# An audio tower on one core: all matmuls on half rows and 32 columns, each half in a PSUM bank of its own, in windows of one exp

## The chip, the cores and the metric

The kernel runs on one core of a Trainium2 chip. The metric is device time in microseconds, the median of several runs; the profile is of one execution. TensorE (PE) multiplies matrices into PSUM, which has 8 banks of 128 partitions x 512 float32. ScalarE (ACT) computes the exponentials, VectorE (DVE) and GpSimd (POOL) the rest, SyncE (SP) issues most DMAs. The engines run beside each other and meet at semaphores.

## The reference

Eight waveforms of 120000 samples go through three layers. `inputs` of the first are frames of 80 samples, 1500 a waveform. Its core:

```python
h = jnp.einsum('bfr,hr->bfh', x, W) + b            # 80 -> 256, then layer norm with gamma, beta
h = gelu_erf(layernorm(h) * ln_gamma + ln_beta)    # "_L0_tok_ref"
h = h + attention(_layernorm(h))                   # 16 heads of 16, 1500 x 1500 scores, Wq Wk Wv Wo, biases
h = h + ffn(_layernorm(h))                         # "_L0_ffn_ref"
```

The last layer would gather 8 // 16 = 0 tokens per head (the leading length, 8, over its 16 heads), so all that is left of it is a layer norm: h + layernorm(layernorm(h)) * ln_g + ln_b. Both kernels compute it so.

## The kernel before

**Tiling.** A batch has 1500 tokens in NT = 12 tiles of T = 125. A chunk is 500 tokens (QC), so NC = 3. A unit is four heads (HG) and one chunk of queries: NU = 12 units a batch, 96 in all. A unit computes, for each of the 12 key tiles and four heads, 125 keys x 500 queries of scores (`scores`, L823; float16 halves of q and k, 64 rows a head, written to a DRAM scratch and read back by `load_group`, L248), their exp on ACT (L486, L489, L494, two heads or 1000 columns each), and the sum with the values (`attend`, L852; float32, 125 rows, four heads in four blocks of 32 columns). Half of each block holds a column of ones, so the row sums come along. No maximum is subtracted unless a check at run time (`take_flag`) asks for a second pass with `exact_max`; with these inputs it isn't run.

**Tiles of the array.** Scores run on 64 rows x 32 columns of the array, in two row halves and four column blocks, eight matmuls a pair of heads. Everything else runs on 128 (125) rows x 32 columns, four matmuls, apart from the transposes (128 x 128). A float32 matmul stands in the trace as two matmul records.

**Rounds.** A unit has PER = 8 rounds of three exps. Scores use banks 0 to 5, three pairs. PE issues three pairs of scores, each after the exp that frees its banks, then one attend (even rounds) or two (odd rounds), then a piece of the next batch or of the last one (`beside`, L860). Attends of unit n go to bank 6 + n % 2, pieces to the other of the two, after DVE has copied out the sums there (`take_sums`, L607).

**Pieces.** A table written by hand (`place`, L37 to L87) says in which unit and round each runs. For the batch after: six token pairs (`tok`, 80 to 256), six transposes of z (`turn`), twelve query or key blocks (`qk`, two halves each), twelve value tiles (`val`), three norm sums (`norm`), one `flag`. For the same or the last batch: twelve output row tiles (`out`). Each has a taker on DVE in the same order: `tok_stats` and `tok_norm` (L513, L522), `take_turn`, `take_qk` (L560), `take_val`, `take_norm`, `take_out` (L625) with its `finish_out` (L635) after the next piece or at the unit's end. Between the two POOL computes the reciprocal root (`out_root`, L382). A piece waits until the piece before it has left its bank (`s_free`).

**Around it.** A unit's sums go from `Osb` by DMA to `thin`, are inverted (`invert`, L613), go back into `Den`, multiply the rest (`normalise`, L617) and go by four DMAs into `oT`. In unit 2, round 2, ACT changes its table and runs the gelu of the whole next batch. Before the loop batch 0's projections run alone; after it the last eight output tiles.

The three exps of a round, and the order of the attends:

```python
act.activation(prob[0:T, 6 * p:6 * p + 2, :], PS[0:T, 0:2, 0:QC], ACT.Exp, scale=scl)
...
if r % 2 == 0:
    attend(n, 3 * q)
else:
    attend(n, 3 * q + 1)
    pe.wait_ge(s_ex, at(s_ex, 3 * R + 3))
    attend(n, 3 * q + 2)
used = beside(b, u, r, bank, used)
```

## Time and profile before

| | us |
|---|---|
| median of 3 runs (2450.72 to 2453.55) | 2451.26 |
| the profiled execution | 2454.76 |
| its span, first to last instruction | 2453.0 |
| first exp to last exp | 117.0 to 2399.1 |
| PE busy (matmuls) | 2220.3 |
| ACT busy | 2153.5 |
| DVE busy | 920.1 |
| POOL busy | 370.5 |

A matmul's time in the trace runs from its start until its last column has left the array, so matmuls that stream side by side or behind each other overlap, and busy PE isn't PE at its peak. Consecutive exps overlap too: each is some 1.0 us long. What one engine can do per unit of time is read from starts, not from lengths. "Idle before" at a line names the engine whose signal ended the idle time. The granted TensorE clock is 0.97 of full speed over the whole span, and 1.00 in most of the loop.

### The profile page before, as it was taken

To read this page: it belongs to the slowest core of one execution; us is meant where nothing else is said; L and a number is where in the kernel's file an instruction comes from. 1 tells how busy PE (TensorE), PEld (TensorE's weight loads), DVE (VectorE), ACT (ScalarE), POOL (GpSimd) and SP (SyncE) were. 2 spreads that over 40 slices of the span, in tenths; PEclk is the share of its full clock that TensorE was granted. 3 is DMA by queue.
4 is the path that set the end of the run, shared out by engine and by line. 5 is a ranking of instruction groups with operands and counts; after the bars stand their busy time and mean duration, and the time that the engine had idled before them with its cause. 6 is when DMAs were issued, how large, how long until landed. Compare 5 with 4: busy or idle time off the path is not lost.

```text
span 2453.0 us, 75572 instructions
## 1 busy us (share of the span) xinstructions
PE 2220.3 (91%) x33324; PEld 613.4 (25%) x33324; DVE 920.1 (38%) x2075; ACT 2153.5 (88%) x2332; POOL 370.5 (15%) x495
## 2 busy tenths in 40 slices
PE   4589999999999999999999999999999999988892
PEld 1222222222222222222222222222222222222221
DVE  7442235532354234533345233542335332330114
ACT  0098999989999899998999899998999989999991
POOL 2211002211021111210112110211112111110002
PEclk7799999999999999999999999999999999999996
DMA  2311221222112222212212221222222122111101
GB/s 71 107 38 40 60 74 41 58 66 67 45 47 67 64 69 49 59 49 59 74 42 51 73 63 45 51 59 64 70 55 51 42 66 69 47 45 39 34 7 32
DMA packets 110030, 135.39 MB, mean 55 GB/s; under 512 B 32263, under 2 KB 89670, under 8 KB 109694
## 3 DMA queue, kind: packets, MB, share of 16 engines
q1 hardware_dynamic: 107158, 128.64, 20.9%
q8 instruction: 264, 4.33, 0.7%
q10 hardware_dynamic: 2536, 1.83, 0.3%
q14 instruction: 72, 0.59, 0.1%
HBM read 55.16 MB, written 61.44 MB: 48 GB/s over the span
## 4 chain that ended last, share of the span: by engine, by line
issue 49%; PE 21%; ACT 14%; POOL 8%; DVE 3%; DMA 2%; POOLq 1%; SPq 1%; DVEq 0%; ACTq 0%
PE PS L856 9%; ACT prob L489 6%; PE PS L830 6%; ACT prob L486 5%; PE PS L790 4%; POOL sq L380 2%; POOL Y L388 2%; ACT prob L494 2%; POOL rs L390 2%; DMA qk_halves_scratch<-HL 1%; SPq L246 1%; DVE HL L568 1%; DVE HL L566 1%; POOLq L389 1%; DVE z L550 1%
## 5 line engine op out<-in xcount | busy, mean ns | idle before, releaser
L856 PE MATMUL PS<-prob,Vst 125*32 125x500 f32 x9216 | 1131.2, 593 | 0.2 <-ACT prob L489 0.2
L494 ACT ACTIVATE prob<-PS 125x1000 f32<-125x1000 f32 x768 | 776.7, 1011 | 133.9 <-PE PS L830 131.8
L486 ACT ACTIVATE prob<-PS 125x1000 f32<-125x1000 f32 x768 | 776.4, 1011 | 80.4 <-PE PS L830 80.4
L830 PE MATMUL PS<-QA,KA 64*32 64x500 f16 (+1 forms) x18432 | 751.9, 381 | 97.5 <-ACT prob L489 48.8
L489 ACT ACTIVATE prob<-PS 125x1000 f32<-125x1000 f32 x768 | 786.7, 1024 | 0.0
L830 PEld LDWEIGHTS PS<-QA,KA 64*32 64x32 f16 (+1 forms) x18432 | 200.5, 90 | 907.3 <-ACT prob L486 416.2
L856 PEld LDWEIGHTS PS<-prob,Vst 125*32 125x32 f32 x9216 | 218.7, 108 | 431.2 <-issue 241.7
L566 DVE TENSOR_SCALAR HL<-PS,b_qk 128x500 f16<-128x500 f32 x96 | 70.9, 738 | 502.9 <-PE PS L790 426.8
L790 PE MATMUL PS<-zT,w_qk 128*32 128x500 f32 x1536 | 197.4, 596 | 9.0 <-DVE Osb L611 7.5
L380 POOL TENSOR_TENSOR sq<-HL 128x2000 bf16<-128x2000 f16 x24 | 84.5, 3520 | 751.4 <-DVE HL L568 751.4
L611 DVE COPY Osb<-PS 128x500 f32<-128x500 f32 x96 | 64.9, 677 | 256.7 <-PE PS L856 256.7
L819 PE MATMUL PS<-w_o,oT 128*32 128x256 f32 (+1 forms) x1536 | 102.5, 388 | 37.1 <-DMA oT<-On 22.4
L799 PE MATMUL PS<-w_v,zT 128*32 128x256 f32 (+1 forms) x1536 | 104.3, 395 | 21.8 <-DVE Vst L573 20.9
L385 POOL TENSOR_SCALAR rs<-mv 125x1 f32<-125x1 f32 x96 | 25.7, 268 | 595.1 <-DVE mv L633 594.5
L623 DVE TENSOR_TENSOR On<-Den,Osb 128x500 f32<-128x500 f32 x96 | 103.7, 1080 | 7.9 <-issue 0.9
L629 DVE TENSOR_TENSOR Hs<-Hs,PS 125x256 f32<-125x256 f32 x96 | 39.6, 413 | 166.2 <-PE PS L819 166.2
L790 PEld LDWEIGHTS PS<-zT,w_qk 128*32 128x32 f32 x1536 | 48.2, 113 | 130.0 <-issue 100.6
L642 DVE SCALAR_TENSOR_TENSOR Y<-Hs,rs,Y 125x256 f32<-125x256 f32 x96 | 72.9, 759 | 7.2
L517 DVE BATCH_NORM_STATS2 st<-PS 125x6 f32<-125x256 f32 x96 | 36.5, 422 | 102.9 <-PE PS L774 102.9
L819 PEld LDWEIGHTS PS<-w_o,oT 128*32 128x32 f32 (+1 forms) x1536 | 46.2, 111 | 113.7 <-issue 36.9
L568 DVE SCALAR_TENSOR_TENSOR HL<-PS,b_qk,HL 128x500 f16<-128x500 f32 x96 | 70.9, 739 | 7.9 <-issue 0.9
L573 DVE TENSOR_TENSOR Vst<-PS,b_v 125x256 f32<-125x256 f32 x96 | 40.1, 421 | 88.5 <-PE PS L799 88.5
(79 smaller groups left out, 961.5 us busy)
## 6 DMA issues: line engine op xcount, KB each, us to landing
qk_halves_scratch<-HL SPq DMA_DIRECT2D x384, 125.0 KB
QA<-qk_halves_scratch SPq DMA_DIRECT2D x64, 375.0 KB, 5.2
KA<-qk_halves_scratch SPq DMA_DIRECT2D x64, 375.0 KB, 7.4
oT<-On SPq DMA_DIRECT2D x384, 31.2 KB, 2.0
out<-Y SPq DMA_DIRECT2D x24, 500.0 KB
X<-in_x SPq DMA_DIRECT2D x8, 468.8 KB, 8.0
thin<-Osb SPq DMA_DIRECT2D x96, 7.8 KB
Den<-thin SPq DMA_DIRECT2D x96, 7.8 KB
```

Of the source, the lines that this page charges most:

```text
L380: pool.tensor_tensor(sq[:, :, :], HL[:, :, 0, :], HL[:, :, 0, :], ALU.mult).then_inc(s_sq, 1)
L486: act.activation(prob[0:T, 6 * p:6 * p + 2, :], PS[0:T, 0:2, 0:QC], ACT.Exp, scale=scl)\
L489: act.activation(prob[0:T, 6 * p + 2:6 * p + 4, :], PS[0:T, 2:4, 0:QC], ACT.Exp, scale=scl)\
L494: act.activation(prob[0:T, 6 * p + 4:6 * p + 6, :], PS[0:T, 4:6, 0:QC], ACT.Exp, scale=scl)\
L566: dve.tensor_scalar(HL[:, i % 4, 0, :], PS[:, bank, 0:QC], bias, None, ALU.add)
L568: dve.scalar_tensor_tensor(out=HL[:, i % 4, 1, :], in0=PS[:, bank, 0:QC], scalar=bias, in1=HL[:, i % 4, 0, :], op0=ALU.add, op1=ALU.subtra ...
L623: dve.tensor_tensor(On[:, :], Den[:, :], Osb[:, :], ALU.mult).then_inc(s_on, 1)
L790: ins = pe.matmul(PS[lo:hi, bank, 0:QC], w_qk[:, c, w, m * 128 + lo:m * 128 + hi], zT[:, c, :], start=(c == 0), stop=(c == KC - 1))
L799: last = pe.matmul(PS[lo:hi, bank, 0:D], zT[:, c, t + lo:t + hi], w_v[:, c, :], start=(c == 0), stop=(c == KC - 1))
L819: last = pe.matmul(PS[lo:hi, bank, 0:D], oT[:, m, e * T + lo:e * T + hi], w_o[:, m, :], start=(m == 0), stop=(m == KC - 1))
L830: last = pe.matmul(PS[lo:hi, bank, 0:QC], KA[rows, G % 2, h // 2, t * T + lo:t * T + hi], QA[rows, G % 2, h // 2, c * QC:(c + 1) * QC], st ...
L856: last = pe.matmul(PS[lo:lo + 2 * HD, 6 + n % 2, 0:QC], Vst[:, b % 2, t, g * HG + j, :], prob[0:T, (HG * t + j) % 12, :], start=(t == 0), ...
```

## The change

Every product that had 125 or 128 rows is cut into rows 0 to 63 and the rest (token frames into 40 samples with the bias row, and 40 from partition 64 on, so `X` and `w_tok` get a second part). Each half writes a bank of its own, four column blocks each, and DVE adds the two banks. Transposes, norm sums and the flag stay as they were. The scores keep their form.

PSUM is divided anew: scores have two pairs of banks (0 to 3) in place of three, attends of unit n use the pair 4 + 2 (n % 2), pieces the other pair.

A unit has WIN = 24 windows, one for each exp. In window k PE waits for exp k - 1, issues the scores of exp k + 1, then in even windows one attend (k // 2 - 1; the unit's last attend is in window 0 of the next unit), in odd windows at most one step of a piece. A token pair, value or output tile has two steps two windows apart, a query or key block four, of half the columns and half the depth each. The table of pieces is new, by window. ACT's wait on `s_pv` is one for every second exp.

On DVE `take_sums`, `invert` and `normalise` stand at windows 1, 7 and 12, `finish_out` three windows after its tile's last step, or at the unit's end. `take_qk` has four operations in place of two and a semaphore of its own (`s_hl`) for the stores and POOL's squares. After the loop the finish of a tile comes behind the take of the next.

```diff
+    RH = RF // 2
...
-    PER = 8
-    assert NU == NT and NT * HG == 6 * PER and KR == 64
...
+    WIN = NT * HG // 2
...
+    OFFSETS = {"tok": (0, 2), "turn": (0,), "qk": (0, 2, 4, 6), "val": (0, 2), "norm": (0,), "flag": (0,), "out": (0, 2)}
+    PLAN = {(u, k): [] for u in range(NU) for k in range(WIN)}
+
+    def place(u, what, *at):
+        for k, i in at:
+            for step, off in enumerate(OFFSETS[what]):
+                PLAN[u, k + off].append((what, i, step, off == OFFSETS[what][-1]))
+
+    place(0, "out", (3, 3), (13, 4), (19, 5))
+    place(0, "tok", (9, 2))
+    place(1, "tok", (3, 3), (15, 4))
+    place(1, "out", (7, 6), (11, 7), (19, 8))
+    place(2, "tok", (3, 5))
+    place(2, "out", (9, 9), (13, 10), (19, 11))
+    place(3, "turn", (3, 0), (5, 1))
+    place(3, "qk", (7, 0), (15, 1))
+    place(4, "qk", (3, 2), (11, 3))
+    place(4, "val", (19, 0))
+    place(5, "val", (3, 1), (7, 2), (11, 3), (21, 4))
+    place(5, "turn", (15, 2), (17, 3))
+    place(5, "norm", (19, 0))
+    place(6, "qk", (3, 4), (11, 5))
+    place(6, "val", (19, 5))
+    place(7, "qk", (3, 6), (11, 7))
+    place(7, "val", (19, 6))
+    place(8, "val", (3, 7), (21, 8))
+    place(8, "turn", (7, 4), (9, 5))
+    place(8, "norm", (11, 1))
+    place(8, "qk", (13, 8))
+    place(9, "qk", (3, 9), (11, 10))
+    place(9, "val", (19, 9))
+    place(10, "qk", (3, 11))
+    place(10, "val", (11, 10), (15, 11))
+    place(10, "tok", (19, 0))
+    place(11, "norm", (3, 2))
+    place(11, "out", (5, 0), (11, 1), (15, 2))
+    place(11, "flag", (9, 0))
+    place(11, "tok", (19, 1))
...
+    NORMS = {(2, 18): 0, (4, 2): 1, (6, 2): 2}
+    GELU = (2, 12)
+
+    TAKE, INVERT, NORMALISE = 1, 7, 12
...
+    def pair(use):
+        if use < FIRST:
+            return 2 * (use % 4)
+        if use < LAST:
+            return 4 + 2 * ((UNIT_OF[use] + 1) % 2)
+        return 2 * ((use - LAST) % 3)
...
-                sp.wait_ge(s_free, at(s_free, USE["qk", b, i] + 1))
+                sp.wait_ge(s_hl, at(s_hl, b * 4 * NC + i + 1))
...
+                        if k == TAKE and n > 0:
+                            spread_sums(n - 1)
+                        if k == INVERT and n > 0:
+                            gather_sums(n - 1)
+                        if k == NORMALISE and n > 0:
+                            store_attended(n - 1)
...
-                            act.wait_ge(s_sc, at(s_sc, 3 * R + 1))
-                            if Q > 0:
-                                act.wait_ge(s_pv, at(s_pv, 3 * Q if p else 3 * Q - 2))
-                            act.activation(prob[0:T, 6 * p:6 * p + 2, :], PS[0:T, 0:2, 0:QC], ACT.Exp, scale=scl)\
-                               .then_inc(s_ex, 1)
-                            act.wait_ge(s_sc, at(s_sc, 3 * R + 2))
-                            act.activation(prob[0:T, 6 * p + 2:6 * p + 4, :], PS[0:T, 2:4, 0:QC], ACT.Exp, scale=scl)\
-                               .then_inc(s_ex, 1)
-                            act.wait_ge(s_sc, at(s_sc, 3 * R + 3))
-                            if Q > 0 and not p:
-                                act.wait_ge(s_pv, at(s_pv, 3 * Q - 1))
-                            act.activation(prob[0:T, 6 * p + 4:6 * p + 6, :], PS[0:T, 4:6, 0:QC], ACT.Exp, scale=scl)\
+                            act.wait_ge(s_sc, at(s_sc, w + 1))
+
+                            if w >= 6 and w % 2 == 0:
+                                act.wait_ge(s_pv, at(s_pv, w // 2 - 2))
+                            act.activation(prob[0:T, 2 * (w % 6):2 * (w % 6) + 2, :],
+                                           PS[0:T, 2 * (w % 2):2 * (w % 2) + 2, 0:QC], ACT.Exp, scale=scl)\
                                .then_inc(s_ex, 1)
 
             second[0] = False
...
+            def tok_stats(b, i):
+                p, e, (upper, lower) = i % 2, hslot(b, 2 * i), two(USE["tok", b, i], slice(0, T), 2 * D)
                 dve.wait_ge(s_full, at(s_full, USE["tok", b, i] + 1))
+                h = Hs[:, e:e + 2, :].rearrange("p a d -> p (a d)")
+                dve.tensor_copy(h, upper)
+                dve.drain()
+                dve.tensor_tensor(h, h, lower, ALU.add).then_inc(s_free, 1)
...
+                upper, lower = two(USE["qk", b, i], slice(0, 128), QC)
+                dve.tensor_scalar(tmp[:, i % 2, :], upper, bias, None, ALU.add)
+                dve.drain()
+                dve.tensor_tensor(tmp[:, i % 2, :], tmp[:, i % 2, :], lower, ALU.add).then_inc(s_free, 1)
+                dve.drain()
+                dve.tensor_copy(HL[:, i % 4, 0, :], tmp[:, i % 2, :])
+                dve.drain()
+                dve.tensor_tensor(HL[:, i % 4, 1, :], tmp[:, i % 2, :], HL[:, i % 4, 0, :], ALU.subtract).then_inc(s_hl, 1)
...
+                dve.tensor_tensor(v, upper, b_v[:, :].rearrange("p (h d) -> p h d", d=HD), ALU.add)
+                dve.drain()
+                dve.tensor_tensor(v, v, lower, ALU.add).then_inc(s_free, 1)
...
-                dve.tensor_copy(Osb[:, :], PS[:, 6 + n % 2, 0:QC]).then_inc(s_ov, 1)
+                bank = 4 + 2 * (n % 2)
+                dve.tensor_copy(Osb[:, :], PS[:, bank, 0:QC])
+                dve.drain()
+                dve.tensor_tensor(Osb[:, :], Osb[:, :], PS[:, bank + 1, 0:QC], ALU.add).then_inc(s_ov, 1)
...
+                dve.tensor_tensor(h, h, upper, ALU.add)
+                dve.drain()
+                dve.tensor_tensor(h, h, lower, ALU.add).then_inc(s_free, 1)
...
+                finish = []
+                for k in range(WIN):
+                    if k == TAKE and n > 0:
+                        take_sums(n - 1)
+                    if k == INVERT and n > 0:
+                        invert(n - 1)
+                    if k == NORMALISE and n > 0:
+                        normalise(n - 1)
+                    if b + 1 < B and (u, k) in NORMS:
+                        norm_stats(b + 1, NORMS[u, k])
+                        norm_apply(b + 1, NORMS[u, k])
+                    for what, pb, i, step, last in pieces(b, u, k):
...
+                            finish.append((k + 3, pb, i))
...
+                    if finish and finish[0][0] == k:
+                        finish_out(*finish.pop(0)[1:])
+                for due, pb, i in finish:
+                    finish_out(pb, i)
...
+            def halves(n):
+                return enumerate((slice(0, 64), slice(64, n)))
...
+                for r, rows in enumerate((slice(0, RH + 1), slice(64, 64 + RH))):
                     for lo, hi in blocks(T):
-                        last = pe.matmul(PS[lo:hi, bank, j * D:(j + 1) * D], X[:, 2 * i + j, lo:hi], w_tok[:, :],
-                                         start=True, stop=True)
...
+                a, c, w, m = step // 2, step % 2, (i % 4) // 2, i % 2
+                if step == 0:
+                    pe.wait_ge(s_free, at(s_free, USE["turn", b, 2 * (i // 4) + 1] + 1))
+                cols = slice(a * QC // 2, (a + 1) * QC // 2)
+                for r, rows in halves(128):
+                    for lo, hi in blocks(128):
+                        last = pe.matmul(PS[lo:hi, bank + r, cols], w_qk[rows, c, w, m * 128 + lo:m * 128 + hi],
+                                         zT[rows, c, cols], start=(c == 0), stop=(c == 1))
...
-                b, g = n // NU, (n % NU) // NC
-                for j in range(HG):
-                    lo = 2 * HD * j
-                    last = pe.matmul(PS[lo:lo + 2 * HD, 6 + n % 2, 0:QC], Vst[:, b % 2, t, g * HG + j, :],
-                                     prob[0:T, (HG * t + j) % 12, :], start=(t == 0), stop=(t == NT - 1))
+                b, g, bank = n // NU, (n % NU) // NC, 4 + 2 * (n % 2)
+                if t == 0:
+                    pe.wait_ge(s_free, at(s_free, UNIT_USES[n]))
+                    if n > 1:
+                        pe.wait_ge(s_ov, at(s_ov, n - 1))
+                for r, rows in halves(T):
+                    for j in range(HG):
+                        lo = 2 * HD * j
+                        last = pe.matmul(PS[lo:lo + 2 * HD, bank + r, 0:QC], Vst[rows, b % 2, t, g * HG + j, :],
+                                         prob[rows, (HG * t + j) % 12, :], start=(t == 0), stop=(t == NT - 1))
...
+                for k in range(WIN):
+                    w = WIN * n + k
+                    if w > 0:
+                        pe.wait_ge(s_ex, at(s_ex, w))
+                    if k < WIN - 1:
+                        scores(w + 1, exact_max)
+                    elif not exact_max and n + 1 < B * NU:
+                        if (u + 1) % NC == 0:
+                            pe.wait_ge(s_ld, at(s_ld, 64 * ((n + 1) // NC + 1)))
+                        scores(w + 1, False)
+                    if k % 2:
+                        beside(b, u, k)
+                    elif k:
+                        attend(n, k // 2 - 1)
+                    elif n > 0:
+                        attend(n - 1, NT - 1)
+
```

Two places in the engines' queues; numbers count an engine's rows. First PE in batch 0, where the query and key blocks of batch 1 begin (before: unit 3, rounds 2 and 3; after: unit 3, windows 6 to 8). "32x500 x3" and "29x500" together are one head's scores, L830 before, L873 after. Before:

```order
468 L856 MATMUL PS<-prob,Vst 32x500 x4
469 L790 MATMUL PS<-zT,w_qk 32x500 x4
470 L830 MATMUL PS<-QA,KA 32x500 x3
471 L830 MATMUL PS<-QA,KA 29x500
...
481 L830 MATMUL PS<-QA,KA 29x500
482 L856 MATMUL PS<-prob,Vst 32x500 x8
483 L790 MATMUL PS<-zT,w_qk 32x500 x4
484 L830 MATMUL PS<-QA,KA 32x500 x3
```

After:

```order
564 L903 MATMUL PS<-prob,Vst 32x500 x8
565 L873 MATMUL PS<-QA,KA 32x500 x3
566 L873 MATMUL PS<-QA,KA 29x500
...
568 L873 MATMUL PS<-QA,KA 29x500
569 L828 MATMUL PS<-zT,w_qk 32x250 x8
570 L873 MATMUL PS<-QA,KA 32x500 x3
...
573 L873 MATMUL PS<-QA,KA 29x500
574 L903 MATMUL PS<-prob,Vst 32x500 x8
```

Before, six heads' scores (rows 470 to 481), three exps' worth, stand between one lump of attends (L856) and half a block (L790) and the next. After, it is two heads' scores, then either an attend (L903, eight matmuls) or a quarter of a block (L828).

Second DVE at the start of unit 1 of batch 1 (batch 1 is the first with outputs of an earlier one), from the sums on. Before, with `take_sums` at L611, a token pair at L517 to L533:

```order
292 L611 COPY Osb<-PS 128x500
293 L517 BN_STATS st<-PS 125x6 x2
294 L519 BN_AGGR mv<-st 125x2
295 L520 BN_AGGR mv<-st 125x2
296 L526 SCALAR_TENSOR_TENSOR Hs<-PS,mv,g_tok 125x256 x2
297 L533 SCALAR_TENSOR_TENSOR Hs<-Hs,rs,be_tok 125x256 x2
...
303 L615 RECIPROCAL thin<-thin 100x20
...
309 L619 STREAM_SHUFFLE Den<-Den 128x500
310 L623 TENSOR_TENSOR On<-Den,Osb 128x500
311 L629 TENSOR_TENSOR Hs<-Hs,PS 125x256
```

After, with the sums at L631 and L633, a token pair at L526 to L545, an output tile from L652 on:

```order
409 L631 COPY Osb<-PS 128x500
410 L633 TENSOR_TENSOR Osb<-Osb,PS 128x500
411 L526 COPY Hs<-PS 125x512
412 L528 TENSOR_TENSOR Hs<-Hs,PS 125x512
413 L531 BN_STATS st<-Hs 125x6 x2
414 L533 BN_AGGR mv<-st 125x2
415 L534 BN_AGGR mv<-st 125x2
416 L540 SCALAR_TENSOR_TENSOR Hs<-Hs,mv,g_tok 125x256 x2
417 L545 SCALAR_TENSOR_TENSOR Hs<-Hs,rs,be_tok 125x256 x2
418 L637 RECIPROCAL thin<-thin 100x20
419 L652 TENSOR_TENSOR Hs<-Hs,PS 125x256
420 L654 TENSOR_TENSOR Hs<-Hs,PS 125x256
```

The sums and the token pair have one operation more over both banks, and the output tiles 6 and 7, which ran in unit 0 before, now stand in this unit.

## Rows read from the trace of the kernel before

**Rows 1.** The page's part 1, busy time, share and instructions of each engine.

```profile
PE 2220.3 (91%) x33324; PEld 613.4 (25%) x33324; DVE 920.1 (38%) x2075; ACT 2153.5 (88%) x2332; POOL 370.5 (15%) x495
```

**Rows 2.** Busy time by stretch, batches 0, 3, 7: five engines, clock, DMA.

```profile
117.00:407.70 290.70, 272.84 (x4069) 73.38 (x4053) 97.48 (x225) 269.29 (x292) 33.48 (x37) 0.97 0.21 51
...
982.00:1269.50 287.50, 273.54 (x4145) 75.21 (x4141) 112.73 (x256) 268.25 (x292) 45.75 (x60) 0.99 0.23 58
...
2131.70:2399.10 267.40, 239.60 (x3639) 60.41 (x3632) 54.88 (x119) 262.79 (x289) 18.89 (x36) 1.00 0.14 31
```

**Rows 3.** Timeline, batch 7: start us, length us, engine, line, operation.

```profile
2205.53 1.01 ACT L489 ACTIVATE prob<-PS 125x1000 f32<-125x1000 f32 x1
...
2208.18 1.05 ACT L489 ACTIVATE prob<-PS 125x1000 f32<-125x1000 f32 x1
...
2208.74 0.95 PE L830 MATMUL PS<-QA,KA 64*32 64x500 f16 x24
...
2209.22 1.00 ACT L494 ACTIVATE prob<-PS 125x1000 f32<-125x1000 f32 x1
```

**Rows 4.** Timeline of PE alone, in batches 1 and 4.

```profile
537.59 0.40 PE L830 MATMUL PS<-QA,KA 64*32 64x500 f16 x8
...
537.92 1.88 PE L856 MATMUL PS<-prob,Vst 125*32 125x500 f32 x16
...
539.62 0.40 PE L806 MATMUL PS<-sq,head_sel 128*32 128x500 bf16 x4
...
1206.27 1.02 PE L790 MATMUL PS<-zT,w_qk 128*32 128x500 f32 x8
...
1207.22 0.61 PE L830 MATMUL PS<-QA,KA 64*32 64x500 f16 x16
```

**Rows 5.** Timeline of VectorE; the last line is a group: busy us, mean ns.

```profile
38.46 0.48 DVE L667 TENSOR_SCALAR w_qk<-w_qk,alpha 128x512 f32<-128x512 f32 x1
...
1212.91 0.74 DVE L566 TENSOR_SCALAR HL<-PS,b_qk 128x500 f16<-128x500 f32 x1 [7.62 <-PE PS L790]
...
1213.72 0.74 DVE L568 SCALAR_TENSOR_TENSOR HL<-PS,b_qk,HL 128x500 f16<-128x500 f32 x1
...
2428.26 0.42 DVE L629 TENSOR_TENSOR Hs<-Hs,PS 125x256 f32<-125x256 f32 x1 [5.90 <-PE PS L819]
...
2429.27 0.18 DVE L633 BATCH_NORM_AGGREGATE mv<-st 125x2 f32<-125x6 f32 x1
...
2431.25 0.48 DVE L639 SCALAR_TENSOR_TENSOR Hs<-Hs,mv,g_ln 125x256 f32<-125x256 f32 x1 [1.79 <-POOL rs L390]
...
L623 DVE TENSOR_TENSOR On<-Den,Osb 128x500 f32<-128x500 f32 x96 | 103.7, 1080 | 7.9 <-issue 0.9
```

**Rows 6.** Timeline of ScalarE around one gelu, batch 3.

```profile
1033.22 1.05 ACT L494 ACTIVATE prob<-PS 125x1000 f32<-125x1000 f32 x1
...
1039.76 1.00 ACT L486 ACTIVATE prob<-PS 125x1000 f32<-125x1000 f32 x1
```

**Rows 7.** Timeline before the loop, VectorE and SyncE's queue.

```profile
18.78 0.76 DVE L517 BATCH_NORM_STATS2 st<-PS 125x6 f32<-125x256 f32 x2
...
21.87 0.76 DVE L517 BATCH_NORM_STATS2 st<-PS 125x6 f32<-125x256 f32 x2
...
70.32 0.74 DVE L566 TENSOR_SCALAR HL<-PS,b_qk 128x500 f16<-128x500 f32 x1 [2.03 <-PE PS L790]
...
79.07 1.40 DVE L541 BATCH_NORM_STATS2 st<-Hs 125x6 f32<-125x256 f32 x4
...
95.99 0.74 DVE L568 SCALAR_TENSOR_TENSOR HL<-PS,b_qk,HL 128x500 f16<-128x500 f32 x1
...
106.62 1.33 SPq L259 DMA_DIRECT2D QA<-qk_halves_scratch  x2
```

**Rows 8.** Timeline of PE after the last exp.

```profile
2426.26 5.92 PE L819 MATMUL PS<-w_o,oT 128*32 128x256 f32 x64 [20.76 <-DMA oT<-On]
```

**Rows 9.** Timeline of PE, value blocks before the loop.

```profile
75.02 3.63 PE L799 MATMUL PS<-w_v,zT 128*32 128x256 f32 x64
```

474 lines of the change are left out of this document (197 added, 277 removed).

## The prediction

> **What bounds the kernel now.** I read the shares first, then the busy time by batch, then the timeline of one quiet unit, then what stands between ScalarE's exps. The shares [rows 1] give TensorE (PE) 91% and ScalarE (ACT) 88%, VectorE (DVE) 38%: two engines near full, so the share settles nothing. The loop over eight batches runs from 117.0 to 2399.1 us, 2282.1 us for 2304 exps; a middle batch takes 287.5, the last, which has little beside its attention, 267.4 [rows 2]. In the last batch three exps start 2.65 us apart, 0.883 each, and that is ACT's own pace; the next start comes 1.04 after its forerunner, 0.48 after the scores that it needed [rows 3]. So ACT's floor for the loop is 2304 x 0.883 = 2034 us, plus seven stops for the gelu of 6.54 - 0.88 = 5.7 us [rows 6], together 2074. The other 208 us are exps that waited, nearly all for scores that stood in PE's queue behind a lump of work: two attends and a piece.
>
> In that queue [rows 4]: one pair of scores streams in 0.61 - 0.40 = 0.21 to 0.22 us. An attend of four float32 matmuls of 500 columns streams in 0.85 (two of them start 1.70 before the piece behind them). That second case is float32 followed by the bfloat16 norm sums on the same tiles (537.92 to 539.62): a change of number format costs nothing. But from the last scores to the attend 0.33 pass in place of 0.22, and from a 500-column half piece back to scores 0.95 in place of 0.85. Each change between 64x32 and 128x32 tiles costs 0.10 to 0.11, sixteen a unit: 1.7 us of PE in each 24 us.
>
> **The change on PE.** A unit is now 24 windows of one exp each (0.883). In each PE does the pair of scores for the next exp, then in an even window one attend, in an odd one nothing or one step of a piece, of 0.42 to 0.43 (half a piece of 0.85, a quarter of a query or key block). All are 64x32, so the sixteen changes go. The attend has 8 tiles of 64 rows in place of 4 of 125 and the same columns a tile. The trace has no float32 on 64-row tiles. Below: the 0.85 of now; above: the two halves one after the other, 1.7. The nearest row is the float16 scores, where 8 such tiles stream side by side in 0.22; I take A = 0.86, today's 0.85 and a little for twice the instructions. Two windows then need 0.22 + 0.86 + 0.22 + 0.43 = 1.73 of ACT's 1.77.
>
> The scores have two buffers, not three. Scores for exp w+1 may start 0.06 after exp w-1 ends (1.01 to 1.05 long) and exp w+1 starts 0.48 behind them. After an attend that chain spans three exps: 1.03 + 0.06 + 0.22 + A + 0.48 = 1.79 + A against 2.65. So an attend is free up to A = 0.86, on the edge. I book 0.1 us a unit, with 0 and 0.5 as bounds: a quiet unit goes from 21.9 to 21.3.
>
> **DVE gets more work**, since it must add the two banks. From [rows 5]: an operation on 500 columns out of PSUM is 0.74, with the gap behind it 0.81; on 256 columns 0.42, or 0.5; on 512 columns in SBUF 0.48. Taking a query or key block grows from 1.6 to 0.81 + 0.81 + 0.55 + 0.6 = 2.8 us and frees the bank after 1.5. A token pair, 3.1 now [rows 7], grows by two 512-column passes to 4.7. An output row tile grows from 1.2 (2428.26 to 2429.45) to 1.7, then waits 1.8 for POOL and needs twice 0.48 with a gap, 1.04, to finish. The sums of a unit go from 0.68 to 1.5. Over the kernel that is 96 x (1.1 + 0.42 + 0.41 + 0.7) + 48 x 1.4 = 320 us, DVE at 1240, half the span. Elsewhere it hides; three places are not hidden, since all pieces of a unit share one pair of banks and the first piece must wait until the last unit's sums have left that pair:
>
> (a) A query or key block, then a piece two windows later. PE wants the bank 1.77 + 0.19 after the last step's start, DVE frees it 0.7 + 1.5 after: 0.45 late, 0.4 at ACT. Eleven a batch: 4.5 us.
> (b) The end of units 0, 1 and 2: an output at windows 19 and 21. Tile ready 1.1 after window 21 opens, 1.7 + 1.8 + 1.04 of DVE and POOL, then the sums 1.5, done 4.5 us into the next unit, while PE wants the bank at 3.06. In units 10 and 11 a token pair (4.7) does the same.
> (c) Units 0 and 1 hold two outputs or more and one or two token pairs. Unit 1's DVE queue is 1.5 + 9.4 + 0.3 + 1.5 + 3 x 4.54 - 1.5 = 25 us long, more than the 21.2 of its exps. I went through it piece by piece (bank free, next step, tile ready, DVE free): unit 11 24.7, unit 0 24.8, unit 1 27.7, unit 2 29.1 with its gelu, unit 3 25.1, units 4 to 10 about 21.9 each. Sum 284, with (a) in it.
>
> Before, the same batch took 287.5. So the middle batches gain only 3.5 us each. Batch 0 has no outputs in units 0 to 2: 268 in place of 290.7. Batch 6 has no token pairs at its end: 281. Batch 7 has only outputs: 256 in place of 267.4. Loop: 268 + 5 x 284 + 281 + 256 = 2225, or 57 less.
>
> **Before the loop** DVE is the chain. Token pairs come 3.09 apart, now 4.65: 6 x 1.56 = 9.4. From a chunk's first block to the next statistics 8.75 pass; now 4 x 2.75 + 4 x 0.94 = 14.8, twice 6. In the last chunk the four blocks take 5 more, but the scratch stores, which lagged by 9.9 behind the last block (95.99 + 0.74 to 106.62) because four of them need 2.4 us against DVE's 1.6, no longer lag: 3 back. Sum +23 [rows 7]: first exp at 140. Bounds 15 (the float32 SBUF passes at half my price, another 2 off each chunk) and 28.
>
> **After the loop** the outputs run a tile every 1.7 + 1.04 = 2.75 instead of 1.2 + 1.8 + 0.98 = 3.95, since the finish now comes one tile later, and inversion and scaling come after two tiles, not four. Last exp to end: 2453.0 - 2399.1 = 53.9 now, and PE starts the last four tiles 27.2 after that exp [rows 1, 2, 8]. Then: sums done 4.5 after the exp (the late output of (b)), two takes, a finish, the inversion, a take, a finish and the scaling, in all 13.6, and some 3.9 for the move into oT as now: 17.5, or 9.7 less. Three more tiles at 2.75 give 3.6 less. 41, or 13 less.
>
> **Sum.** 140 + 2225 + 41 = 2406, plus 1.8 around the span = 2408 against 2454.8 of the profiled run, which lies 3.5 above the median. So 2405 us, 1.9% faster.
>
> **A rule against it.** [rows 9]: 64 matmuls in 3.63 us, 51 to 57 ns each, is the densest long run shown; there the columns alone ask for 53. The changed kernel has about 50,900 matmul records in place of 33,324, and a busy pair of windows holds 48 in 1.77 us, 37 ns each, which no row shows kept up. If PE could take only one per 51 ns, such a pair would last 2.45, the loop's 49,400 records 2520 and the whole some 2700. The Trainium skill, "TensorE: Matmul & The Clock Gate", section "Wait — 56ns, not 53.3ns?", says that with hardware decode off the sequencer spends about 62 ns per matmul; by that the loop would be 50,900 x 62 = 3156 us. The 51 ns of the row already lie under it, but a queue filled earlier could explain that.
>
> **Rivals.**
> 1. Forecast: PE's changes are gone, ACT's pace binds in 7 units of 12, DVE in the rest. 2405, its own range 2375 to 2440. Chance 0.50.
> 2. The attend crosses its edge (slower). On 8 float32 tiles A is not 0.86 but more; every even window that DVE doesn't hold up pays the excess, some 8 of 12 units, 12 x 64 = 770 windows and part of the others, say 900. From A = 0.91 the gain of 46 is gone; at 0.95 the time is 2405 + 80 = 2485; one change of float kind costing 0.1 each way, as tile changes do now, gives over 2550. Against: float32 to bfloat16 costs nothing. Chance 0.17.
> 3. Issue of matmuls binds, above: 2500 to 2700. Chance 0.06.
> 4. DVE's waits hide better than I walked: the waits for POOL overlap, SBUF passes are quicker. (b) and (c) halved are 10 us a batch: 2335; gone entirely 2290. Chance 0.19.
> 5. The tile changes go but float32 in halves and DVE's new waits just balance them: 2447 to 2456. Chance 0.04, and 0.04 for DVE beyond my walk (POOL slows it; it is the reason why one 500-column product averages 1080 ns where another takes 0.68 [rows 5]): 2470.
>
> What a measurement can tell from no change is about 0.2%, 5 us. Faster holds 1, 4 and a little of 2: 0.72. Same 0.05, slower 0.23. The range leaves out the far half of 4's and 2's ends and 3: 2330 to 2490.
>
> **What would show it.** Right: L903 attends starting 0.22 after scores, and the next scores 0.85 to 0.87 behind them; quiet units of the last batch 21.2 to 21.5; first exp near 140; DVE near 1240 us; middle batches 280 to 288 with idle ACT in the first windows of units 0 to 3, released by scores behind DVE's Osb sum; tail near 41. Wrong: quiet units over 22 (rival 2 or 3; a matmul start-to-start of over 35 ns would say 3), or middle batches under 275 (rival 4), which would make DVE's waits smaller than my walk has them.

## The result and the profile after

The changed kernel takes 2509.52 us (median of 4 runs, 2507.19 to 2514.93) against 2450.99 beside it: a ratio of 1.024, 95% interval 1.0221 to 1.0258. It is 2.4% slower, 58 us. The prediction said 2405, within 2330 to 2490.

The page's busy times of the changed kernel, with columns as in [rows 1], then its busy time by stretch for batches 0, 3 and 7, as in [rows 2]:

```profile
PE 2092.9 (84%) x50988; PEld 855.7 (34%) x50988; DVE 1207.5 (48%) x2651; ACT 2154.3 (86%) x2332; POOL 371.5 (15%) x495
```

```profile
139.44:418.16 278.72, 249.22 (x6133) 99.38 (x6125) 128.42 (x280) 268.04 (x291) 32.48 (x35) 0.98 0.22 55
1012.61:1310.23 297.62, 260.36 (x6373) 107.55 (x6373) 149.58 (x330) 270.37 (x293) 45.78 (x60) 0.97 0.22 57
2201.73:2461.21 259.48, 218.51 (x5016) 70.46 (x5016) 65.72 (x147) 258.78 (x289) 18.19 (x36) 1.00 0.14 33
```

Against [rows 2], batch 7 became 8 us shorter (267.4 to 259.5), batch 0 12 us shorter, and each of the six between them about 10 us longer (batch 3: 287.5 to 297.6). So where VectorE has little beside the attention the change is a gain. From the first exp to the last the kernel loses 40 us (2282.1 to 2321.8), in the batches with all their pieces. Before the loop it loses 22.4 (the first exp starts at 139.4, before at 117.0), and behind it it gains 9.7 (from the last exp's end to the end of the span 44.2 us pass, before 53.9).

A quiet pair of windows in batch 7, TensorE alone (start, length, engine, line; idle time in brackets):

```profile
2280.85 0.41 PE L873 MATMUL PS<-QA,KA 64*32 64x500 f16 x8 [0.34 <-ACT prob L498]
2281.07 1.02 PE L903 MATMUL PS<-prob,Vst 64*32 64x500 f32 x16
2281.91 0.40 PE L873 MATMUL PS<-QA,KA 64*32 64x500 f16 x8
2282.64 0.40 PE L873 MATMUL PS<-QA,KA 64*32 64x500 f16 x8 [0.34 <-ACT prob L498]
```

The attend follows the scores after 0.22 and holds TensorE 0.84 us (2281.07 to 2281.91). In eight tiles of 64 rows it takes no longer than in four of 125 (0.85, [rows 4]). A quiet unit takes 21.5 us.

What a middle batch loses: each unit from the start of its first exp to the next unit's, us, mean of batches 1 to 5, beside the prediction's walk.

| unit | 11 | 0 | 1 | 2 | 3 | 4 to 9 | 10 | batch |
|---|---|---|---|---|---|---|---|---|
| predicted | 24.7 | 24.8 | 27.7 | 29.1 | 25.1 | 131.4 | 21.9 | 284 |
| measured | 23.9 | 25.6 | 28.4 | 30.8 | 29.1 | 134.7 | 25.4 | 298 |

The predicted units as the walk lists them add up to 284.7, not 284.

Some of TensorE's waits for VectorE over the whole run (line, what it waited for: us in total, times, longest):

```profile
PE PS L815 <- DVE Osb L633: 22.3, 6, 4.0
PE PS L805 <- DVE Osb L633: 21.4, 11, 2.6
PE PS L837 <- DVE tmp L581: 20.8, 46, 1.6
PE PS L837 <- DVE Vst L593: 18.2, 7, 2.6
```

L633 is the second half of take_sums, L581 and L593 are the adds that free the bank of a query or key block and of a value tile. The first line is the start of unit 3; here it is in batch 3, VectorE's timeline and then TensorE's:

```profile
1098.16 0.48 DVE L664 SCALAR_TENSOR_TENSOR Hs<-Hs,mv,g_ln 125x256 f32<-125x256 f32 x1
1098.71 2.43 DVE L667 SCALAR_TENSOR_TENSOR Y<-Hs,rs,Y 125x256 f32<-125x256 f32 x1
1101.07 0.41 DVE L652 TENSOR_TENSOR Hs<-Hs,PS 125x256 f32<-125x256 f32 x1
...
1104.54 0.48 DVE L664 SCALAR_TENSOR_TENSOR Hs<-Hs,mv,g_ln 125x256 f32<-125x256 f32 x1 [1.79 <-POOL rs L403]
1105.10 0.48 DVE L667 SCALAR_TENSOR_TENSOR Y<-Hs,rs,Y 125x256 f32<-125x256 f32 x1
1105.50 0.67 DVE L631 COPY Osb<-PS 128x500 f32<-128x500 f32 x1
1106.25 0.67 DVE L633 TENSOR_TENSOR Osb<-Osb,PS 128x500 f32<-128x500 f32 x1
```

```profile
1102.89 0.42 PE L873 MATMUL PS<-QA,KA 64*32 64x500 f16 x8
1106.98 1.09 PE L815 MATMUL PS<-ident,z 125*128 125x125 f32 x4 [3.66 <-DVE Osb L633]
```

and ScalarE's next exp:

```profile
1108.69 1.00 ACT L498 ACTIVATE prob<-PS 125x1000 f32<-125x1000 f32 x1 [4.33 <-PE PS L873]
```

The last output tile of unit 2 is taken at 1101.07, VectorE then idles 1.79 for GpSimd's root, finishes the tile, and only then takes the sums. TensorE has stood still for 3.66 us at its first piece, with the scores that ScalarE needs queued behind it. Two more things show. L667 took 2.43 us in place of 0.48. And behind the stop the granted clock is low, 0.51, and the attend that follows takes 1.74 us in place of 1.02 (columns as in [rows 2]):

```profile
1106.40:1109.80 3.40, 2.82 (x28) 1.26 (x36) 1.20 (x2) 1.00 (x1) 0.00 (x0) 0.51 0.02 2
```

### The profile page after: what moved, and what is told of

It is laid out like the page before. It is cut to its first block, busy times and chain, and to the rows that moved or that the text cites. A ratio compares the mean times of both kernels' runs of the same rounds, so it can differ in the third digit from the quotient of the medians.

```text
span 2505.4 us, 112108 instructions
## 1 busy us (share of the span) xinstructions
PE 2092.9 (84%) x50988; PEld 855.7 (34%) x50988; DVE 1207.5 (48%) x2651; ACT 2154.3 (86%) x2332; POOL 371.5 (15%) x495
## 4 chain that ended last, share of the span: by engine, by line
issue 37%; PE 33%; ACT 10%; POOL 9%; DVE 7%; POOLq 1%; DMA 1%; DVEq 1%; SPq 0%; ACTq 0%
PE PS L903 15%; ACT prob L498 10%; PE PS L873 9%; PE PS L828 6%; POOL Y L401 3%; DVE tmp L581 2%; DVE tmp L579 2%; POOL rs L403 2%; PE PS L837 2%; PE PS L815 1%; POOL sq L393 1%; POOL rs L374 1%; POOLq L402 1%; POOL Hs L387 1%; DVEq L580 0%
## 5 line engine op out<-in xcount | busy, mean ns | idle before, releaser
L498 ACT ACTIVATE prob<-PS 125x1000 f32<-125x1000 f32 x2304 | 2111.1, 1049 | 266.0 <-PE PS L873 249.0
L903 PE MATMUL PS<-prob,Vst 64*32 64x500 f32 (+1 forms) x18432 | 1219.3, 590 | 9.0 <-DVE Hs L654 7.5
L873 PE MATMUL PS<-QA,KA 64*32 64x500 f16 (+1 forms) x18432 | 962.4, 381 | 152.4 <-ACT prob L498 138.5
L873 PEld LDWEIGHTS PS<-QA,KA 64*32 64x32 f16 (+1 forms) x18432 | 273.9, 91 | 1068.1 <-ACT prob L498 986.3
L903 PEld LDWEIGHTS PS<-prob,Vst 61*32 61x32 f32 (+1 forms) x18432 | 363.0, 107 | 72.9 <-issue 12.3
L828 PE MATMUL PS<-zT,w_qk 64*32 64x250 f32 x6144 | 236.9, 378 | 16.1 <-DVE tmp L581 14.4
L579 DVE TENSOR_SCALAR tmp<-PS,b_qk 128x500 f32<-128x500 f32 x96 | 70.9, 738 | 302.8 <-PE PS L828 260.0
L393 POOL TENSOR_TENSOR sq<-HL 128x2000 bf16<-128x2000 f16 x24 | 84.5, 3520 | 727.9 <-DVE HL L585 727.9
L848 PE MATMUL PS<-w_o,oT 64*32 64x256 f32 (+1 forms) x3072 | 128.9, 403 | 45.3 <-DVE Osb L633 14.7
L837 PE MATMUL PS<-w_v,zT 64*32 64x256 f32 (+1 forms) x3072 | 127.7, 385 | 44.5 <-DVE tmp L581 20.8
L631 DVE COPY Osb<-PS 128x500 f32<-128x500 f32 x96 | 64.9, 676 | 194.2 <-PE PS L903 194.2
L828 PEld LDWEIGHTS PS<-zT,w_qk 64*32 64x32 f32 x6144 | 113.8, 107 | 84.5 <-DVE tmp L581 30.1
L591 DVE TENSOR_TENSOR Vst<-PS,b_v 125x256 f32<-125x256 f32 x96 | 40.6, 423 | 154.2 <-PE PS L837 154.2
L645 DVE TENSOR_TENSOR On<-Den,Osb 128x500 f32<-128x500 f32 x96 | 85.9, 895 | 7.9 <-issue 0.9
L652 DVE TENSOR_TENSOR Hs<-Hs,PS 125x256 f32<-125x256 f32 x96 | 39.6, 412 | 94.0 <-PE PS L848 94.0
L815 PE MATMUL PS<-ident,z 125*128 125x125 f32 x192 | 37.3, 331 | 49.2 <-DVE z L562 26.9
L526 DVE COPY Hs<-PS 125x512 f32<-125x512 f32 x48 | 33.1, 689 | 81.9 <-PE PS L805 81.6
```

The source lines that it names most:

```text
L393: pool.tensor_tensor(sq[:, :, :], HL[:, :, 0, :], HL[:, :, 0, :], ALU.mult).then_inc(s_sq, 1)
L498: act.activation(prob[0:T, 2 * (w % 6):2 * (w % 6) + 2, :], PS[0:T, 2 * (w % 2):2 * (w % 2) + 2, 0:QC], ACT.Exp, scale=scl)\
L579: dve.tensor_scalar(tmp[:, i % 2, :], upper, bias, None, ALU.add)
L631: dve.tensor_copy(Osb[:, :], PS[:, bank, 0:QC])
L645: dve.tensor_tensor(On[:, :], Den[:, :], Osb[:, :], ALU.mult).then_inc(s_on, 1)
L828: last = pe.matmul(PS[lo:hi, bank + r, cols], w_qk[rows, c, w, m * 128 + lo:m * 128 + hi], zT[rows, c, cols], start=(c == 0), stop=(c == 1))
```

## The experiments

**1. What the adds cost.** In every taker the pass over the second bank is left out; for a query or key block:

```diff
-                dve.tensor_scalar(tmp[:, i % 2, :], upper, bias, None, ALU.add)
-                dve.drain()
-                dve.tensor_tensor(tmp[:, i % 2, :], tmp[:, i % 2, :], lower, ALU.add).then_inc(s_free, 1)
+                dve.tensor_scalar(tmp[:, i % 2, :], upper, bias, None, ALU.add).then_inc(s_free, 1)
```

> The changed kernel, with every VectorE operation that adds the second bank left out (token pairs, query and key blocks, value and output tiles, sums), so half of each sum is missing from the output. TensorE, ScalarE and GpSimd do the same work in the same order. Theory A (the stalls of units 0 to 3, 10 and 11 are TensorE waiting for VectorE's queue, which the added operations lengthened): the middle batch falls from 298 to 270-280 us, the first exp to about 120, the whole to 2310-2380. Theory B (the stalls come from the order of the pieces and from GpSimd, whatever VectorE has to do): the middle batch stays above 290 and only the 20 us before the loop are saved, 2480 or more.

2364.4 us, 145 less than the changed kernel. Batch 3, columns as above:

```profile
954.91:1231.71 276.80, 255.82 (x6373) 103.55 (x6373) 119.31 (x276) 266.53 (x294) 45.32 (x60) 0.98 0.24 61
```

The first exp starts at 126.8, 12.6 earlier (not 20 as expected), and a middle batch takes 277.5 in place of 297.9, as Theory A had it. Without VectorE's added passes the change would be a gain of 87 us; with them it is a loss of 58. But 14 us of stalls a batch (277.5 less twelve quiet units of 21.5 and the gelu's 5.6) stay even without them.

**2. The sums ahead of what is left over.** `late` holds what a piece still needs at a unit's end:

```diff
                         take_sums(n - 1)
+                        while late:
+                            what, *args = late.pop(0)
+                            what(*args)
...
                 for due, pb, i in finish:
-                    finish_out(pb, i)
+                    late.append((finish_out, pb, i))
```

and so for tok_norm of a token pair whose last step is at window 21.

> The changed kernel with one part of VectorE's order altered: what a late piece has left to do at a unit's end (finish_out, tok_norm) is done behind the next take_sums, not ahead of it. The same operations. Theory A (the sums stand behind GpSimd's root, 1.8 us, and the finish, 1.04, or behind the 1.6 us of a token pair's norm, and the next unit's first piece waits for them): the stalls at windows 3 to 5 of units 11, 0, 1, 2 and 3, now 1.3, 3.7, 3.7, 2.2 and 7.4 us in a middle batch, shrink by 2 to 4 us each in units 0, 2 and 3 and by about 1.5 in 11 and 1; 8 to 12 us a batch, whole time 2425-2450. Theory B (the queue as a whole is too long in units 0 to 3, so that what is saved at the start is waited for later in the same unit): under 4 us a batch, 2480 or more.

2432.9 us, a ratio of 0.992 to before: the same work in a better order takes 77 us away, and this version is 0.8% faster than the kernel before (interval 0.9893 to 0.9951). A middle batch takes 285.9, 12.0 less. Unit 0 went from 25.6 to 22.2, unit 1 from 28.4 to 25.2, unit 3 from 29.1 to 24.5. Little of it was waited for later: window 12 of unit 1 grew by 0.24 us, and unit 10 went from 25.4 to 26.2.

**3. GpSimd's long operations moved.**

```diff
                                 root2(b + 1, NORMS[u, k])
-                                add_bias(b + 1, NORMS[u, k])
+                                if NORMS[u, k]:
+                                    add_bias(b + 1, NORMS[u, k])
+                            if b + 1 < B and (u, k) == (3, 7):
+                                pool.wait_ge(s_rc, at(s_rc, b * NU + u))
+                                add_bias(b + 1, 0)
...
+                                    if i == NT - 1:
+                                        pool.wait_ge(s_on, at(s_on, b * NU + u))
                                     squares(pb, i // 4)
```

> The changed kernel, with two long GpSimd operations moved away from VectorE's operations on two SBUF operands: the 3.52 us of squares in unit 10 start only behind normalise, and the 2.54 us of bias addition of the next batch's first chunk moves from unit 2 to unit 3, behind invert. In the trace VectorE's L645 took 3.40 us beside the one and L667 2.43 beside the other, where 0.68 and 0.48 are usual. Theory A (VectorE is held while GpSimd uses the same SBUF path, and TensorE's 2.6 us wait for the value block in unit 10 is that): unit 10 falls from 25.5 to about 22.5, unit 3 from 29.1 to 27; 5 us in each of seven batches, 2465-2475. Theory B (the long L645 is a result of something else that moves along): nothing changes, 2500 to 2510.

2472.5 us, the median of eight runs, 37 less. In the profiled one a middle batch takes 290.8, 7.1 less; but that one was the fastest of the eight (2461.0), and by the medians it is 37 us over seven batches, 5.3 each. Unit 10 went from 25.4 to 21.9, unit 3 from 29.1 to 26.9, as Theory A had it. What was there in the changed kernel (unit 10 of batch 3), VectorE, then GpSimd:

```profile
1272.59 0.74 DVE L641 STREAM_SHUFFLE Den<-Den 128x500 f32<-128x500 f32 x1
1273.40 3.40 DVE L645 TENSOR_TENSOR On<-Den,Osb 128x500 f32<-128x500 f32 x1
1276.72 0.41 DVE L591 TENSOR_TENSOR Vst<-PS,b_v 125x256 f32<-125x256 f32 x1
```

```profile
1272.74 3.52 POOL L393 TENSOR_TENSOR sq<-HL 128x2000 bf16<-128x2000 f16 x1 [56.08 <-DVE HL L585]
```

L645 starts while GpSimd works and ends when GpSimd is done (1276.80 and 1276.26). With the squares behind it, L651 of the third experiment is the same product in 0.68:

```profile
1275.92 0.68 DVE L651 TENSOR_TENSOR On<-Den,Osb 128x500 f32<-128x500 f32 x1
```

**4. The attends in whole rows, in the new windows.**

```diff
-                for r, rows in halves(T):
+                for r, rows in ((0, slice(0, T)),):
```

with one bank in take_sums.

> The changed kernel with the attends of the whole 125 rows in four matmuls in one bank, as before the change, in the new windows; take_sums copies one bank. Everything else is in halves. Theory A (a change between tile shapes costs 0.10 to 0.11 us on TensorE, and a pair of windows has next to nothing to spare): each attend costs two changes, 0.2 us, a quiet unit of the last batch goes from 21.5 to 23.5-24, the loop is 100 to 200 us longer where VectorE doesn't bind anyway, whole time 2580-2660. Theory B (the halves cost in TensorE what the changes did, since eight tiles stream no faster than four): quiet units 21 to 22 and a time of 2490 to 2510, a little less through the shorter sums.

2596.4 us, 87 more than with halves, though VectorE had one pass of 0.67 us less to do in each unit. TensorE in batch 7:

```profile
2421.94 0.40 PE L871 MATMUL PS<-QA,KA 64*32 64x500 f16 x8 [0.20 <-ACT prob L498]
2422.28 1.04 PE L901 MATMUL PS<-prob,Vst 125*32 125x500 f32 x8
2423.25 0.93 PE L871 MATMUL PS<-QA,KA 64*32 64x500 f16 x16
```

The attend starts 0.34 after the scores and holds TensorE 0.97, where halves show 0.22 and 0.84: 0.12 and 0.13 for the two changes. A quiet unit takes 22.4, less than the 23.5 to 24 expected: of 0.25 for each of twelve attends, 3 us, a third reaches ScalarE. Theory A's mechanism and its whole time (2580 to 2660) hold, its size in a quiet unit was too large.

**5. The old kernel with the new load on VectorE.** The same operation is done twice, as here for the sums, with similar lines in the other takers:

```diff
+                dve.tensor_copy(Osb[:, :], PS[:, 6 + n % 2, 0:QC])
+                dve.drain()
                 dve.tensor_copy(Osb[:, :], PS[:, 6 + n % 2, 0:QC]).then_inc(s_ov, 1)
```

> The kernel before the change, with VectorE's load of the changed one: operations on the same data are done twice (per query or key block one of 500 and one of 256 columns more, 1.3 us; per token pair two statistics, per value tile, output tile and per unit's sums one more). TensorE keeps whole rows, three pairs of scores and its rounds; the output is unchanged. Theory A (the added VectorE work costs as much wherever a piece waits for it; the halves themselves gained 0.4 us a quiet unit and no more): the middle batch rises from 287.5 by 12 us or more, 2530 or above. Theory B (in the old rounds one piece follows three exps behind the last, so VectorE has time, and three pairs of scores cover a wait; the load hurts only in the new windows, where a piece follows after 1.77 us and a wait of any length reaches ScalarE): under 4 us a batch in the loop and about 20 before it, 2470 to 2495.

2597.7 us. VectorE is at 1224.6 us, near the changed kernel's 1207.5. Its page:

```profile
PE 2234.5 (86%) x33324; PEld 606.3 (23%) x33324; DVE 1224.6 (47%) x2651; ACT 2153.8 (83%) x2332; POOL 375.8 (14%) x495
```

Theory A holds in this: the old rounds hide the load no better, and a middle batch goes from 287.6 to 305.5. Its aside that the halves gained no more than 0.4 us a quiet unit does not hold, as the table shows that this makes with the first experiment, medians in us:

| | VectorE's old load | VectorE's new load |
|---|---|---|
| whole rows, rounds of three exps | 2451.0 | 2597.7 |
| half rows, windows of one exp | 2364.4 (adds left out) | 2509.5 |

The kernel before measured 2450.9 to 2454.5 in the four comparisons. The halves and windows gain 87 in the one column and 88 in the other; the load costs 147 in one row and 145 in the other. In these four kernels the two parts of the change add up, and the second is the larger. It is not shown that they must: the load is paid in different places (in the old rounds 9.7 of the 18 us a batch lie in units 4 to 9, in the windows 3.8 of 20), and the ninth experiment shows that its price depends on the order. (The loads of a column aren't quite equal: VectorE is busy 920.1 and 966.1 us in the left one, 1224.6 and 1207.5 in the right one, and the first experiment keeps the new casts and copies.)

**6 and 7. The order mended further.** In 6, experiments 2 and 3 together, and an output's finish always behind the next piece's take. In 7, also four windows between a query or key block and the next piece, in units 4, 6, 7 and 9:

```diff
-    place(4, "qk", (3, 2), (11, 3))
-    place(4, "val", (19, 0))
+    place(4, "qk", (3, 2), (13, 3))
+    place(4, "val", (21, 0))
```

> The changed kernel with VectorE's order altered in three ways and the same operations: an output tile's finish stands behind the next piece's take, not ahead of it; what is left at a unit's end stands behind the sums (as in the second experiment); the squares of unit 10 and the first bias addition are moved as in the third. Theory A (all the stalls of units 0 to 3, 10 and 11 are a bank that VectorE empties late, because it waits for GpSimd's root or is held by GpSimd's long operations): the second experiment's 286 us a batch less 7 us for the port and 3 to 5 for the finishes, 275; whole time 2345 to 2375. Theory B (VectorE's sheer amount of work in units 0 to 3): the 25 us of stalls left in these units move but stay, 2395 or more.

> As the run before it, and in units 4, 6, 7 and 9 the second query or key block begins at window 13 in place of 11 and the value tile at 21 in place of 19, so that there are four windows between one block's last step and the next block's first. Theory A (the 0.33 + 0.17 us at windows 12 and 13 of these units are VectorE's two passes of 1.5 us over a block's two banks against TensorE's 1.77): this stall goes in four units, 0.5 us each, seven times, 14 us in all, and the one at window 20 stays (now at 22). Theory B (a fixed cost of beginning a piece): nothing changes by more than 3 us.

2389.4 and 2381.3 us. The sixth lies between the two theories, 14 above the range of A and 6 below B's 2395: a middle batch takes 279.7 (275 by Theory A), and unit 3 stayed at 26.2. So these three edits do not take all the stalls away. The seventh saved 8, not 14, and the runs of the two nearly meet (2386 to 2393, and 2374 to 2387). In its profile the stalls at windows 12 and 13 went in all four units (0.5 to 0.6 us each), but unit 5 took 0.5 more. In the changed kernel this wait looks so:

```profile
1137.28 0.40 PE L873 MATMUL PS<-QA,KA 64*32 64x500 f16 x8
1138.05 0.66 PE L828 MATMUL PS<-zT,w_qk 64*32 64x250 f32 x16 [0.37 <-DVE tmp L581]
```

**8. The one place that was left.** In the sixth, VectorE at the end of unit 2:

```profile
1049.79 1.38 DVE L568 TENSOR_SCALAR z<-Hs,mv,rs 125x256 f32<-125x256 f32 x4 [1.53 <-POOL rs L380]
1051.08 0.41 DVE L658 TENSOR_TENSOR Hs<-Hs,PS 125x256 f32<-125x256 f32 x1
...
1054.92 0.68 DVE L639 TENSOR_TENSOR Osb<-Osb,PS 128x500 f32<-128x500 f32 x1
```

An output tile waits through GpSimd's root. So norm_apply goes behind its take:

```diff
                         norm_stats(b + 1, NORMS[u, k])
-                        norm_apply(b + 1, NORMS[u, k])
+                        if NORMS[u, k]:
+                            norm_apply(b + 1, NORMS[u, k])
...
+                    if b + 1 < B and (u, k) == (2, 21):
+                        norm_apply(b + 1, 0)
```

> As the run with the gap behind query and key blocks, and on VectorE the normalisation of the next batch's first chunk (norm_apply, four passes) stands behind the take of the last output tile of unit 2, not ahead of it. In the trace of the run before VectorE idled 1.54 us for GpSimd's root there, with that tile waiting, and the sums of unit 2 were done 2.5 us into TensorE's wait. Theory A (the order at this one place costs 2 to 3 us a batch): the stalls at windows 4 and 5 of unit 3 fall from 3.5 to about 1, whole time 15 to 20 us lower, near 2363. Theory B (the transposes of unit 3 then wait for z in place of the sums): less than 5 us.

2364.4 us, 17 less, as Theory A had it, unit 3 from 26.1 to 23.3. Its ratio to before is 0.9636 (0.9616 to 0.9657): 3.6% faster than the kernel before with the same operations on TensorE and VectorE as the changed one. VectorE at the same place:

```profile
1036.68 0.38 DVE L562 BATCH_NORM_AGGREGATE mv<-st 125x2 f32<-125x6 f32 x4
1037.02 0.42 DVE L658 TENSOR_TENSOR Hs<-Hs,PS 125x256 f32<-125x256 f32 x1
...
1040.13 1.37 DVE L568 TENSOR_SCALAR z<-Hs,mv,rs 125x256 f32<-125x256 f32 x4
1041.43 0.67 DVE L637 COPY Osb<-PS 128x500 f32<-128x500 f32 x1
```

**9. The adds once more, in the mended order.**

> As the run beside it, without the adds of the second bank (half of every sum is missing from the output). Theory A (what the adds still cost in the loop, once VectorE's order is right, is the 0.4 us behind each query or key block and a rest in units 0 to 3): the middle batch is 4 to 8 us shorter than in the run beside it, in place of the 20 that the first experiment showed, and 19 us are saved before the loop: whole time 45 to 75 us less. Theory B (the adds cost what they cost in any order): 20 us a batch again, 140 us or more.

2303.1 us, 61 less, as Theory A had it; 15 of them lie before the loop, 19 expected. A middle batch takes 268.1 against 275.0: in this order the adds cost 6.9 us a batch in the loop, where they cost 20.4 in the order of the change. So two thirds of the adds' price in the loop went with the edits of experiments 2, 3 and 6 to 8, and one third stayed.

## Why the prediction was wrong

**What bounds the kernel, and TensorE's side: right.** The attend in halves takes 0.84 (predicted 0.86), a quiet unit 21.5 (21.2 to 21.5), the last batch 259.5 (256). The fourth experiment shows that the changes of tile shape cost what was read, for the attends. Rival 2 is out. So is rival 3. In unit 4 of batch 3 a pair of windows with a piece in it:

```profile
1131.06 1.02 PE L903 MATMUL PS<-prob,Vst 64*32 64x500 f32 x16
1131.90 0.40 PE L873 MATMUL PS<-QA,KA 64*32 64x500 f16 x8
1132.11 0.62 PE L828 MATMUL PS<-zT,w_qk 64*32 64x250 f32 x16
1132.63 0.40 PE L873 MATMUL PS<-QA,KA 64*32 64x500 f16 x8
1132.85 1.02 PE L903 MATMUL PS<-prob,Vst 64*32 64x500 f32 x16
```

These are 48 matmul records from 1131.06 to 1132.85, 37 ns each, at the pace of a quiet pair. The Trainium skill ("TensorE: Matmul & The Clock Gate", section "Wait — 56ns, not 53.3ns?") gives about 62 ns per matmul for hardware decode off. This trace shows 37 ns a record in its place; which decode path these runs used, none of them shows. (The prediction's sum for the loop by that rule took the 50,900 records of the whole kernel for the loop's 49,400.)

**Before the loop: right in size.** 22.4 us later, predicted 23; by the first experiment 12.6 of them are the adds. The other 9.8 were not taken apart; what else is new there are the copies and casts of the takers, and the halves. **After the loop:** 44.2, predicted 41. A tile takes 3.09 (takes at 2488.72 and 2491.81), not 2.75, and in each L667 takes 1.04 beside a GpSimd operation, where 0.48 is usual:

```profile
2487.76 1.04 DVE L667 SCALAR_TENSOR_TENSOR Y<-Hs,rs,Y 125x256 f32<-125x256 f32 x1
2488.72 0.41 DVE L652 TENSOR_TENSOR Hs<-Hs,PS 125x256 f32<-125x256 f32 x1
...
2491.81 0.41 DVE L652 TENSOR_TENSOR Hs<-Hs,PS 125x256 f32<-125x256 f32 x1
```

**DVE gets more work, terms (b) and (c): wrong, and this is the step that failed.** The loop took 2321.8, predicted 2225: 97 us. The prediction expected TensorE to wait for VectorE's sums in units 11 and 0 to 3, and it does; what it had too small is the walk of VectorE's queue in the middle batches, by 13.9 us a batch (298 against 284). It had unit 10 quiet (21.9), and that unit measured 25.4. The excess, in parts that overlap:

- 5.3 to 7.1 of them, by the third experiment, are VectorE held by GpSimd's long operations: 3.5 in unit 10, 2.2 in unit 3. The walk priced every VectorE operation at its undisturbed time. The sign was in the trace of before: [rows 5] has a mean of 1080 ns for the product that takes 0.68 alone. The prediction read that row, and put it into a rival of 4% and 2470 us, not into the sum. Over the whole run the two kinds of operation that are held took 64.7 us more than at their median length in the kernel before, and only 35.8 in the changed one. So the hold did not grow; it now stands where TensorE waits for what comes behind it.
- (b) had the sums of unit 2 done 4.5 us into unit 3. In the trace they are done at 1106.92, and unit 3's first exp starts at 1098.95: 8.0 us. The walk names neither norm_stats nor norm_apply, which stand on VectorE's queue just there with a wait of their own for GpSimd's root, 1.56 us, nor the held L667 (2 us, in the item above too). Unit 3 measured 29.1 for 25.1, and 24.5 once the sums were taken first (experiment 2).
- 1.7 us of exps that waited in windows 14 to 17 of unit 2, behind the gelu, at a lower clock, see below. Without the adds, in the ninth experiment, they are still there.
- About 1 us at window 6 of unit 5 without any semaphore, see below.
- Units 4 to 9 took 134.7 for 131.4: a quiet unit is 21.5 and not 21.3, and the item of unit 5.

A stop also costs more than its own length, since the clock falls behind it. In the loop of the changed kernel the granted clock was at the lower level for 126 us, in the kernel before for 38, in the eighth experiment for 44. Of the 126 only 48 lie in unit 2, with its gelu; the rest lie in units 0, 1, 3 and 10, where TensorE stands still for VectorE. The prediction has no term for it, and what it adds was not measured apart.

(a) came near by luck: the walk's own numbers, 0.7 + 1.5 less 1.77 + 0.19, give 0.24 us late and not the 0.45 that it booked. ScalarE lost 0.3 to 0.4, with 0.17 more at the next exp.

The range was wrong for the same reason: beyond the walk it had one cause, "POOL slows it", at 2470, where several pushed the same way. The table of experiment 5 says what a better sum would have been: in the first experiment the adds cost 125.5 us in the loop (2321.8 less 2196.3), 12.6 before it and 4 behind it. A middle batch has 30 us of adds (VectorE busy 149.6 less 119.3), and 20.4 of them reached ScalarE.

The loss comes from the added passes in this order, and taking away either is enough: without the adds the kernel is 145 us faster (experiment 1), and with all of them in a better order (of VectorE's queue, of two GpSimd operations and of a few pieces), VectorE busy 1193.7 us against 1207.5, it is 145 us faster too (experiment 8).

## What to carry to other kernels

When a change gives an engine more work that "hides", list for every buffer who waits for its release, and put the releasing operation ahead of everything on that queue that itself waits for a third engine. Before making buffers shallower (here two pairs of scores for three), look for waits in the feeding queue that are longer than the spare time: here one wait of 3.66 us stopped ScalarE for 4.33. And where an operation's mean is well above its shortest, find what holds it, and whether it will stand on the path after the change.
